# Cross attention, a state-space scan and experts on one core: first layers of three pairs ahead of the norm, and a first turn with its own order

## What is computed

```
x = x + xattn(hidden = ctx, z = layernorm(x))
x = x + ffn(layernorm(x))

xattn: xc = causal conv of 4 taps over (in_proj_w @ ctx);  u = silu(xc + conv_b)
       dt_lo, B, C = x_proj_w @ u
       delta = softplus(dt_proj_w @ dt_lo + dt_proj_b);  A = -exp(A_log)      # 16 states
       state = state * exp(delta * A) + (delta * u) * B;  y = sum_n state * C  # scan over 256 steps
       y = (y + D * u) * silu(z)
ffn:   shared = (sum over 2 experts of relu(x @ w1 + b1) @ w2 + b2) / 2
       routed = sum over 32 experts of gate * (relu(x @ w1 + b1) @ w2 + b2)    # width 176, top 6 of softmax
```

## Time and profile before

| | |
|---|---|
| median of 3 runs | 382.17 us |
| the profiled execution | 382.66 us, of which the span from first to last instruction is 380.8 |
| PE matmul busy | 354.3 us, 93% |
| DVE busy | 268.0 us, 70% |
| ACT busy | 218.9 us, 57% |
| POOL busy | 201.8 us, 53% |
| mean granted clock of PE | 0.978 of full speed |
| last product of batch 0's scan | starts at 54.61 us |
| first layer of pair 0, batch 0 | starts at 68.73 us |

### The profile page before, as it was taken

The page is one execution under the profiler, slowest core; times in us unless marked ns, Lnnn a source line. Parts: engine busy times, 40 slices in busy tenths (PEclk is TensorE's granted clock), DMA queues, the critical chain, the costliest instruction groups (busy, mean ns, idle before and its releaser), DMA issues.

```text
span 380.8 us, 6888 instructions
## 1 busy us (share of the span) xinstructions
PE 354.3 (93%) x2293; PEld 319.9 (84%) x2293; DVE 268.0 (70%) x455; ACT 218.9 (57%) x545; POOL 201.8 (53%) x159
## 2 busy tenths in 40 slices
PE   7437689999999999999999999999999998999997
PEld 4224367899999989999999899999999898999996
DVE  2579888999999547699977566899763645454454
ACT  2578764777864436477644446496424346665662
POOL 0289997178996102389962002799830033445442
PEclk9958899999999999999999999999999999999999
DMA  7498761159623223898322144964222144333310
GB/s 223 141 308 251 248 213 59 56 188 309 209 79 84 83 59 103 231 323 224 102 83 83 55 118 160 328 217 140 83 84 83 43 146 117 100 86 91 104 57 28
DMA packets 30825, 54.26 MB, mean 142 GB/s; under 512 B 3306, under 2 KB 8654, under 8 KB 30798
## 3 DMA queue, kind: packets, MB, share of 16 engines
q1 hardware_dynamic: 30798, 53.93, 46.9%
HBM read 52.60 MB, written 1.31 MB: 142 GB/s over the span
## 4 chain that ended last, share of the span: by engine, by line
PE 81%; DVE 8%; POOL 5%; issue 2%; ACT 2%; DMA 1%; SPq 0%; DVEq 0%; POOLq 0%; ACTq 0%
PE acc L552 36%; PE z L574 12%; PE z L576 11%; PE z L575 11%; PE dA L552 4%; POOL bu L957 3%; POOL w1l L937 2%; DVE dA L792 2%; PE misc L472 1%; DVE cv L756 1%; PE acc L450 1%; PE dA L486 1%; DMA ctxT<-in_ctx 1%; PE misc L526 1%; DVE b2F L776 1%
## 5 line engine op out<-in xcount | busy, mean ns | idle before, releaser
L552 PE MATMUL acc<-hg,w 128*128 128x256 f32 x564 | 133.5, 379 | 0.0
L712 ACT ACTIVATE z<-z,par 128x256 f32<-128x256 f32 x188 | 75.8, 439 | 82.8 <-PE z L576 82.5
L574 PE MATMUL z<-xh,w1l 128*128 128x256 f32 (+1 forms) x376 | 118.1, 314 | 0.0
L552 PEld LDWEIGHTS acc<-hg,w 128*128 128x128 f32 x564 | 102.4, 190 | 11.2
L957 POOL TENSOR_TENSOR bu<-bt,du 128x512 f32<-128x512 f32 x64 | 81.0, 1278 | 54.7 <-DMA bt<-bc 37.0
L894 DVE TENSOR_TENSOR hg<-z,gt 128x512 f32<-128x512 f32 x88 | 60.5, 688 | 64.9 <-ACT z L712 63.7
L576 PE MATMUL z<-xh,w1h 128*128 128x256 f32 (+1 forms) x376 | 106.2, 282 | 0.0
L575 PE MATMUL z<-xl,w1h 128*128 128x256 f32 (+1 forms) x376 | 105.9, 282 | 0.0
L792 DVE TENSOR_TENSOR_SCAN dA<-dA,bu 128x512 f32<-128x512 f32 x64 | 78.2, 1222 | 6.6 <-POOL bu L957 6.0
L574 PEld LDWEIGHTS z<-xh,w1l 128*128 128x128 f32 x376 | 71.2, 189 | 3.8 <-issue 2.2
L575 PEld LDWEIGHTS z<-xl,w1h 128*128 128x128 f32 x376 | 70.8, 188 | 1.6
(11 more groups left out here) (135 smaller groups left out, 410.0 us busy)
## 6 DMA issues: line engine op xcount, KB each, us to landing
w<-in_w SPq DMA_DIRECT2D x92, 256.0 KB, 2.8
bt<-bc SPq DMA_DIRECT2D x32, 256.0 KB, 5.0
ct<-bc SPq DMA_DIRECT2D x32, 256.0 KB, 5.7
stage<-in_w SPq DMA_DIRECT2D x11, 512.0 KB, 6.1
gt<-gates SPq DMA_DIRECT2D x14, 128.0 KB
xr<-in_xr SPq DMA_DIRECT2D x4, 256.0 KB, 6.1
x<-in_xT SPq DMA_DIRECT2D x4, 256.0 KB, 4.9
out<-x SPq DMA_DIRECT2D x3, 256.0 KB, 6.9
```

What stands on the lines that cost most here:

```text
L552: mm = pe.matmul(total(b, k), weights, h, start=t + n == 0 and (k == 0 or final_batch(b)), stop=last, skip_group_check=True)
L574: pe.matmul(z[p % ZB][:, i, :], w1l[:, t, one], xh_, start=k == 0, stop=False)
L712: ins = act.activation(z[p % ZB][:, i, :], z[p % ZB][:, i, :], ACT.Relu, bias=b1[:, t:t + 1])
```

## The change

- **First layers early.** For pairs 0 to 2 of batch 0 the first layer is computed from the centred xc, before the root of the variance is known (steps "xch" and "xcl" split it, "l1" is the first layer). When the root n2 is there, DVE multiplies z by it ("zr"), and the ReLU follows. Pair 3 is the first with the normed x.
- **Shared pairs.** For pairs 0 and 1 of every batch ACT writes hg itself (scale 1/2 and a halved bias b1s); DVE's product falls away.
- **The loop is written out.** run() goes over all batches and pairs. Turn 0 has a table of its own, TURN0; the units stand beside pairs 3 to 15 (UNIT_AT), two of them beside pairs 6, 10 and 13. The copying part of "turn" is a step of its own, "gates_out": beside pair 6 in batch 0. b2 is added behind second layer 6 there instead of 4.
- **Head.** Four products of batch 0 (POOLED) go from DVE to POOL, with their states in hg. The lower parts of w1 chunks 2 to 5 (BY_PE) are made by PE, identity times stage minus identity times w1h, in z1 and z2, and copied to w1l by ACT ("w1p", "w1e"). The first row pair of B is broadcast by PE ("rows") and ACT ("bt0") instead of through DRAM. delta of batch 0 is made in two halves; nb1 goes to ACT; the sum over the states of half k = 1 goes to misc, so that x1 of half 0 waits only for its own half. 39 fewer warm matmuls (of 78) stand before the norm.
- econv of batch 1 goes to the PSUM tile acc (e_of).

The core of the diff:

```diff
+EARLY = 3
 B2_AT = 4
+B2_AT0 = 6
 GLOW_AT = 2
+GLOW_AT0 = 6
 SINGLE0 = NP - NPR
 
 
 BURING = 4
+POOLED = [3, 6, 8, 11]
+BY_PE = [2, 3, 4, 5]
...
 BACK = [("yfold", 16), ("x1", 17), ("x1s", 18), ("mean", 19), ("centre", 19), ("sq", 19), ("sqs", 19), ("var", 20), ("r2", 20), ("norm", 20), ("logits", 21),
-        ("xh", 21), ("xl", 21), ("top", 21), ("ex", 22), ("gates", 22), ("turn", 23)]
-THIS = UNITS + ZGATE + BACK
+        ("xh", 21), ("xl", 21), ("top", 21), ("ex", 22), ("gates", 22), ("turn", 23), ("gates_out", 23)]
 NEXT = [("xin", 14), ("cv0", 15), (("taps", 1, KC), 16), ("econv", 17), ("uclip", 17), ("usig", 18), ("u", 19), ("xall", 20),
         ("dtl", 21), ("dt", 21), ("sp", 22), ("over", 22), ("delta", 23)]
-BEHIND = ("var", "logits", "xall", "dt", "turn")
+TURN = [(n, at, 1) for n, at in UNITS + ZGATE + BACK] + [(n, at, 2) for n, at in NEXT]
+BEHIND = ("var", "logits", "xall", "dt", "turn", "spread")
+AHEAD = [("xall", 1), ("var", 1)]
+
+
+UNIT_AT = [3, 4, 5, 6, 6, 7, 8, 9, 10, 10, 11, 12, 13, 13, 14, 15]
+TURN0 = [(("bu", 0, 0), 2, 1), (("bu", 0, 1), 2, 1)]
+for _c in range(NC):
+    for _k in range(KD):
+        _u = 2 * _c + _k
+        TURN0 += [(("decay", _c, _k), max(UNIT_AT[_u] - 1, 3), 1), (("scan", _c, _k), UNIT_AT[_u], 1), (("prod", _c, _k), UNIT_AT[_u], 1)]
+        TURN0 += [(("bu", (_u + 2) // 2, _k), UNIT_AT[_u], 1)] if _c + 1 < NC else []
+        TURN0 += [(("fold", _c, _k), UNIT_AT[_u], 1)]
+TURN0 += [("stats", 4, 1), ("rs1", 5, 1), ("nb1", 6, 1), ("zz", 7, 1), ("ez1", 8, 1), ("ez2", 9, 1), ("ez3", 10, 1), ("zmul", 12, 1),
+          ("xin", 15, 2), ("cv0", 15, 2), ("yfold", 15, 1), (("taps", 1, 2), 16, 2), ("x1", 16, 1), ("x1s", 16, 1),
+          (("taps", 2, 3), 17, 2), (("taps", 3, KC), 17, 2), ("econv", 17, 2), ("uclip", 18, 2), ("usig", 18, 2), ("u", 19, 2),
+          ("mean", 20, 1), ("centre", 20, 1), ("sq", 20, 1), ("sqs", 20, 1), ("xall", 20, 2), ("var", 21, 1), ("dtl", 21, 2), ("dt", 21, 2),
+          ("r2", 21, 1), ("norm", 21, 1), ("xh", 22, 1), ("logits", 22, 1), ("xl", 22, 1), ("sp", 22, 2), ("over", 22, 2), ("top", 22, 1),
+          ("ex", 23, 1), ("gates", 23, 1), ("delta", 23, 2), ("turn", NP, 1), ("gates_out", NP, 1)]
...
 HEAD = [(("warm", None, 11), 0), ("xin", 0), (("warm", None, 16), 0), ("cv0", 0), (("taps", 1, KC), 0), (("warm", "conv_done", 6), 0), ("econv", 0), ("uclip", 0),
-        (("warm", "uclip_done", 8), 0), ("usig", 0), ("b2h", 0), ("w1h", 0), ("w1l", 0), (("warm", "usig_done", 4), 0), ("u", 0), ("stats", 0), ("b2l", 0), ("xall", 0),
-        ("dtl", 0), ("b2s", 0), ("w1h", 0), ("w1l", 0), ("dt", 0), ("sp", 0), ("over", 0), ("rs1", 0), ("w1h", 0), ("delta", 0), ("nb1", 0)]
+        (("warm", "uclip_done", 8), 0), ("usig", 0), ("b2h", 0), ("w1h", 0), ("w1l", 0), (("warm", "usig_done", 4), 0), ("minus", 0), ("u", 0), ("stats", 0), ("b2l", 0), ("xall", 0),
+        ("dtl", 0), ("b2s", 0), ("w1h", 0), ("w1l", 0), ("dt", 0), ("rows", 0), ("sp", 0), ("over", 0), ("bt0", 0), ("delta", 0)]
 HEAD += [(("bu", 0, _k), 0) for _k in range(KD)]
 for _c in range(NC):
     HEAD += [(("decay", _c, _k), 0) for _k in range(KD)]
     HEAD += [(("bu", _c + 1, _k), 0) for _k in range(KD)] if _c + 1 < NC else []
-    HEAD += [("w1l", 0)] if _c in (1, 3, 5, 6, 7) else []
-    HEAD += [(n, 0) for n in ((), (), ("zz",), ("ez1",), ("ez2",), ("ez3",), ("zmul",), ())[_c]]
-    HEAD += [("w1h", 0)] if _c in (1, 2, 4, 5) else []
+    HEAD += [("w1l", 0)] if _c == 7 else []
+    HEAD += [("w1p", 0)] if _c in (1, 2, 4, 5) else []
+    HEAD += [("w1e", 0)] if _c in (2, 3, 5, 6) else []
+    HEAD += [(n, 0) for n in (("rs1", "nb1"), (), ("zz",), ("ez1",), ("ez2",), ("ez3",), ("zmul",), ())[_c]]
+    HEAD += [("w1h", 0)] if _c in (0, 1, 2, 4, 5) else []
     HEAD += [("xin", 1), ("cv0", 1)] if _c == NC - 1 else []
     for _k in range(KD):
         HEAD += [(("scan", _c, _k), 0), (("prod", _c, _k), 0)]
     HEAD += [(("sum", _c - 1), 0)] if _c else []
-HEAD += [("w1h", 0), ("w1l", 0), (("warm", None, 12), 0), (("sum", NC - 1), 0), ("w1h", 0), ("w1l", 0), ("w1h", 0), ("w1l", 0),
+HEAD += [("w1h", 0), ("w1l", 0), (("sum", NC - 1), 0), ("w1h", 0), ("w1l", 0), ("w1h", 0), ("w1l", 0),
          (("taps", 1, 2), 1), (("warm", None, 22), 0), ("w1h", 0), ("x1", 0), ("mean", 0), (("warm", None, 13), 0), (("taps", 2, 3), 1),
-         ("centre", 0), ("sq", 0), ("w1l", 0), (("taps", 3, KC), 1), ("var", 0), ("econv", 1), ("uclip", 1), ("r2", 0),
-         (("warm", None, 31), 0), ("norm", 0), ("usig", 1), ("xh", 0), ("logits", 0), ("w1h", 0), ("w1l", 0), ("u", 1), ("xl", 0),
-         ("top", 0), ("ex", 0), ("xall", 1), ("gates", 0), ("dtl", 1)]
-OPEN = [[("dt", 1), ("sp", 1), ("over", 1), ("delta", 1)],
-        [("spread", 0), ("turn", 0)],
-        [("acc_free", 0)] +
-        [(n, 1) for n in (("bu", 0, 0), ("decay", 0, 0), ("bu", 0, 1), ("decay", 0, 1), ("bu", 1, 0), ("scan", 0, 0), ("prod", 0, 0),
-                          ("decay", 1, 0), ("bu", 1, 1), ("scan", 0, 1), ("prod", 0, 1), ("decay", 1, 1), ("scan", 1, 0),
-                          ("prod", 1, 0), ("fold", 1, 0), "stats")]]
+         ("centre", 0), ("sq", 0), ("xch", 0), ("w1l", 0), (("taps", 3, KC), 1), ("xcl", 0), ("var", 0), (("warm", None, 4), 0),
+         (("l1", 0), 0), (("l1", 1), 0), (("l1", 2), 0), ("econv", 1), ("w1h", 0), ("w1l", 0),
+         ("uclip", 1), ("r2", 0), ("norm", 0), (("zr", 0), 0), ("usig", 1), ("xh", 0), ("logits", 0), ("xl", 0), ("u", 1),
+         ("top", 0), (("zr", 1), 0)]
+OPEN = [[("ex", 0), ("gates", 0), (("zr", 2), 0)],
+        [("dtl", 1)],
+        [("gt0", 0), ("sp", 1), ("over", 1), ("delta", 1)],
+        [("xall", 1), ("dt", 1), ("spread", 0)],
+        [],
+        [("turn", 0)],
+        [("gates_out", 0)]]
...
+            def beside(b, p):
+                due = list(OPEN[p]) if first(b) and p < len(OPEN) else []
+                for i in range(B - 1):
+                    due += [(n, i + d) for n, at, d in (TURN if i else TURN0) if i * NP + at == b * NP + p and i + d < B]
+                return due
 
             for name, b in HEAD:
                 step(name, b)
-            for p in range(SKEW):
-                pair(0, p, OPEN[p])
-            with eng.Fori(0, B - 2) as i:
-                for p in range(SKEW, NP):
-                    pair(i, p, beside(i, p))
-                for p in range(SKEW):
-                    pair(i + 1, p, beside(i + 1, p))
-            for p in range(SKEW, NP):
-                pair(B - 2, p, beside(B - 2, p, later=False))
-            for p in range(SKEW):
-                pair(B - 1, p, [])
-            for p in range(SKEW, NP):
-                pair(B - 1, p, [])
+            for b in range(B):
+                for p in range(NP):
+                    pair(b, p, beside(b, p))
...
-            load_bc(1, 0)
-            load_bc(1, 1)
+            for c in range(BRING):
+                load_bc(1, c)
             for b in range(B):
                 eng.wait_ge(S["gates_done"], b + 1)
                 eng.dma_start(gates_d[b % 2], gT[0:NR, :]).then_inc(S["spilled"], 16)
                 eng.wait_ge(S["spilled"], 16 * b + 16)
                 if b:
-                    eng.wait_ge(S["hg_done"], (b - 1) * NP + SINGLE0 + NPART)
+                    wait_hg(eng, b - 1, SINGLE0 + NPART - 1)
                     load_gates(b, 0)
-                    eng.wait_ge(S["hg_done"], b * NP)
+                    wait_hg(eng, b - 1, NP - 1)
                 load_gates(b, 1)
                 for p in range(NP):
-                    if b == 0 and p < 2:
-                        load_bc(1, 2 + p)
                     if 0 < b < B - 1 and p < BRING - 1:
...
+            lower = list(BY_PE)
+
+            def lower_w1(i):
+                pe.wait_ge(S["minus_done"], 1)
+                pe.wait_ge(w1h_done, i + 1)
+                if BY_PE.index(i):
+                    pe.wait_ge(w1e_done, BY_PE.index(i))
+                high = w1h[:, i * WCH:(i + 1) * WCH, :].rearrange("p t m -> p (t m)")
+                for h in range(2):
+                    for j in range(2):
+                        part = slice((2 * h + j) * L, (2 * h + j + 1) * L)
+                        pe.matmul(z[1 + h][:, j, :], ident, stage[:, i % WRING, part], start=j == 0, stop=False, skip_group_check=True)
+                    for j in range(2):
+                        part = slice((2 * h + j) * L, (2 * h + j + 1) * L)
+                        mm = pe.matmul(z[1 + h][:, j, :], minus[:], high[:, part], start=False, stop=True, skip_group_check=True)
+                mm.then_inc(S["w1p_done"], 1)
+
             def step(name, b):
-                if name[0] == "sum":
+                if name == "w1p":
+                    lower_w1(lower.pop(0))
+                elif name[0] == "l1":
+                    if name[1] == 0:
+                        pe.wait_ge(S["xcl_done"], 1)
+                    first_layer(name[1], xh[:, 1], xl[:, 1])
...
+                elif name == "rows":
```

(69 more changed lines are left out.)

165 lines of the change are left out of this document (104 added, 61 removed).

## The result

The changed kernel takes 388.52 us (median of 4 runs, 388.24 to 389.55) where the kernel before takes 382.17 (381.36 to 382.26, 4 runs): a ratio of 1.0175, 95% interval 1.0163 to 1.0187. The forecast was 385.9 with a range of 380.5 to 389.0, and "slower" with a chance of 0.75. The profiled execution took 388.61 us with a span of 386.8, so 6.0 more than the span of before.

The account below looks back on a forecast made before the run. TensorE's stream, busy 93% of the span, was taken as the bound. -0.65 (head) - 4.16 (to second layer 6) + 6.6 (w2 wait) + 0.24 (b2) + 1.7 (clock) = +3.7 on 382.17 gives 385.9 us, range 380.5 to 389.

Parts of the forecast that it names:

- C: Mark from which times are counted: the end of "centre" of batch 0, at 60.85 us in the kernel before.
- head, up to C: Start of batch 0 up to the end of "centre": 0.65 us earlier, with ACT's sum of work carrying it.
- C to second layer 6, unhindered: Batch 0 from C to the second layer of pair 6, without the weight wait: 4.16 us earlier than now.
- wait for w2 of pair 6: TensorE waits ahead of second layer 6 of batch 0 for its late weight load: 6.6 us, bounds 5.0 to 7.8.
- b2 and clock: b2 moved behind second layer 6 adds 0.24 us; half clock after the weight wait adds 1.7, bounds 0 and 2.8.
- the order on ACT: gates_out stands behind ReLU 6, decay 4 and product 2, so gates_done comes at C + 30.1 and delays the load.
- the bound of 2.0: Quickest landing time in us taken for the pair 6 w2 load, giving the low wait of 5.0; 2.8 was assumed.
- the walk: Unit-by-unit pricing of the batch 0 head: last decay ready at 51.8, last product at 54.7, C earlier by 0.65.
- The price of 1.0 for a half clock that lasts one stretch longer: Upper bound for the head: C comes 1.0 us later if the half clock lasts one stretch more.
- it costs nothing more: Coupling recurs at units 9 and 13, costing DVE some 2 us each, but hg of pair 14 comes when PE asks.
- rival one: The w2 load for pair 6 comes in time, so no wait: -4.6 us, 377.6 us; chance 0.13.
- Small moves and the loop: hg of pairs 0 and 1 on ACT, the bt(0,0) row by PE and ACT, and the written-out loop: nothing gained.

Follow-up runs that it names:

- experiment 1: Changed kernel with the w2 loads of pairs 6 to 8 of batch 0 issued by SP before the gates transfer; 389.86 us, ratio 1.0221.
- experiment 2: Changed kernel with decays 4, 9 and 13 of batch 1 listed on ACT under their own pair; 382.88 us, ratio 1.0033.
- experiment 7: Kernel of experiment 2 without the early first layers of pairs 0 to 2, warm matmuls in their place; 387.57 us, ratio 1.0117.
- experiment 8: Kernel of experiment 2 with all 16 products of the head on DVE, none on POOL; 388.48 us, ratio 1.0181.
- experiment 5: Kernel of experiment 2 with DVE's chain to u of batch 2 taken forward, u in pair 18 instead of 19; 383.52 us, ratio 1.0028.
- experiment 4: Kernel before the change with only its loop over two batches written out; 382.02 us, ratio 0.9999.
- experiment 10: Kernel of experiment 9 with 50 more warm matmuls ahead of the first lower part of w1; 381.01 us, ratio 0.9976.
- experiment 9: Kernel of experiment 6 with 12 warm matmuls behind sum(3) in the head; 381.35 us, ratio 0.9981.
- experiment 11: Kernel of experiment 9 without the early first layers of pairs 0 to 2; 385.89 us, ratio 1.0074.
- experiment 3: Changed kernel with both the w2 loads ahead of the gates and the three decays under their own pair; 384.23 us, ratio 1.0080.
- experiment 6: Kernel of experiment 5 with the w2 loads of pairs 6 to 8 issued ahead of the gates; 381.61 us, ratio 0.9991.
- experiment 12: Kernel of experiment 9 with all 16 products of the head on DVE; 383.02 us, ratio 1.0025.

## Why the prediction was right, and where it was not

The time is 2.6 us above the forecast of 385.9. The terms of the sum, in the profiled executions (C as in the prediction; after, C is 58.46 + 0.70 = 59.16):

| term | forecast | measured | from |
|---|---|---|---|
| head, up to C | -0.65 | -1.69 | 60.85 to 59.16 |
| C to second layer 6, unhindered | -4.16 | -3.82 | 95.33 to 89.82, less the head |
| wait for w2 of pair 6 | +6.6 | +8.17 | idle ahead of 97.99 |
| b2 and clock | +0.24 + 1.7 | +1.68 | 4.84 instead of 3.16 to second layer 7 |
| up to here | +3.7 | +4.34 | 102.83 against 98.49 |
| wait for u of batch 2 | 0 | +2.2 | second layer 18, 142.74 against 136.19 |
| wait behind the gates of batch 1 | 0 | +0.9 | 164.37 against 156.95 |
| batches 1 to 3 | 0 | -1.4 | 219.14 against 220.57 |

**What held.** The forecast hinged on the order on ACT: gates_out behind a ReLU, behind a decay, behind product 2. Product 2 was due at C + 27.35 and ended at C + 27.6; gates_done was due at C + 30.1 and came at C + 30.3; second layer 3 was due at C + 20.8 and came at C + 21.1. The shape too: a hole ahead of second layer 6, the gates sent 12.2 us behind du of batch 1, half clock behind it. Only the releaser was named otherwise, hg instead of the DMA, and experiment 1 shows that it was the DMA.

**The size of the wait.** SP was quicker than taken (load issued at C + 33.2, not 34.2), the load slower. It was given 2.8 us by the median in the earlier trace rows; it took 5.5. The five w2 loads issued from 92.3 to 98.4 take 5.5, 6.7 and 7.0 us (min, median, max). This could have been read before: in the trace of the kernel before, the load of pair 6 itself, issued at 81.99 among the broadcasts of B and C, took 6.6 us, and all seven of 80 to 100 a median of 5.8. The median over 96 loads was the wrong row, and the bound of 2.0 too. But the broadcasts behind the load don't set its time alone: with the same transfers issued behind it, the first five at the same distances, it took 3.0 us in experiments 2 and 7, 4.5 in 8 and 5.1 in 5. Why is open.

**The head.** Forecast -0.65, measured -1.69, of which 0.70 lies ahead of the first delta (20.61 to 19.91; it starts between 19.3 and 20.1 in the changed kernels and at 20.06 in the kernel of experiment 4, so this part is mostly no effect of the change) and 0.99 in the scan. So the walk was near, and its reason stood the test of experiment 10 (ACT, not the half clock in the first lower part). The price of 1.0 for a half clock that lasts one stretch longer holds: 0.55 in experiment 9, 0.95 in 5. What the bound left out is a second stretch in the queue ahead of a sum, 1.6 more in experiments 5 and 7.

**The step that failed** is "it costs nothing more". The prediction saw that decays 9 and 13 repeat the coupling and cost DVE some 2 us each (measured: idle 2.28 and 1.17, beside 2.19 for pair 6). It then asked only whether hg of pair 14 comes late, and didn't follow DVE's chain to its end, u of batch 2, on which xall hangs. Before, u is done at 130.75 and TensorE asks for it at 133.67: 2.9 us to spare, less than the change takes out of TensorE's stream (5.5 at second layer 6), while du is no earlier than before (77.29 against 75.67). Hence rival one (377.6 if the load comes in time) could not have come true with this order: experiment 1 removes the load's wait, and the time stays. The prediction's number was near because two limits of nearly the same length lay one under the other and it had found one of them. That much of it is luck: the +6.6 stands for a wait that is really there but doesn't set the end of the turn, in the place of a limit that the prediction didn't see.

**Small moves and the loop.** Nothing, as forecast: experiment 4, 0.9999.

**What stays open.** From batch 1 on, all changed kernels take 219.1 us between the marks and both forms of the kernel before 220.6 to 220.9. Of the 1.4 us 1.0 lies in batch 3, where the second layer is split: most of its second layers lie 2.86 apart before, and 2.78 and 2.84 in turn after. In batches 1 and 2 they lie 3.15 apart instead of 3.16. It is not the loop and not the chip (experiments 1, 2 and 4 ran on the same one). What makes the matmuls quicker I haven't found. The wait for x of batch 0 at batch 1 (0.7 to 1.3 in every changed kernel) was not tried: gates_out of batch 1 stands under pair 0 of the next batch there.

**A version that beats both.** Decays beside their own pair, u early, w2 first, warm matmuls in the head (experiment 10): 381.01, 0.24% below the kernel before (interval 0.13% to 0.35%) and 2.0% below the changed kernel by the ratios (0.9976 against 1.0175). It keeps every part of the change. How much of the profit is the early layers' isn't shown (experiment 11).

## What to carry to other kernels

When a change pulls the bounding engine's stream forward, write down for each other engine's chain how much it had to spare before; the gain at that point is capped by the smallest of these (here 2.9 us at u), and a hole that you find may hide a second limit as long as itself. Take one hole away at a time and look where the end of the chain behind it lies, not only whether the hole is gone. In an in-order queue, an entry that waits for the same step's work of another engine passes its wait to everything behind it: three entries moved by one place were worth 5.4 us, more than the early layers or POOL's share of the products brought here. And take the price of a transfer from the row of that very transfer, not from the median of its kind: 6.6 us against 2.8.

## What the runs showed of the hardware

- The same head runs with a first stretch at half clock of 10.2 us (18.9 to 29.1, changed kernel) or 13.7 us (17.7 to 31.3, experiment 5), and with or without a second one. A wait of TensorE of 1.95 us (experiments 5 and 7) was followed by a second stretch of 3.4 us, one of 1.50 in the same place (changed kernel, experiments 1, 2, 3 and 6) was not, and, behind 12 warm matmuls, neither was one of 1.86 (experiment 12). The longer first stretch moves the end of the head by 0.55 to 0.95 us, the second one by 1.6. In other places too equal waits differ: one of 3.38 us was followed by half clock in experiment 3 and not in experiment 1 (1.00 from 139.5 to 144), one of 1.8 in experiment 6 and not in experiment 9 (1.00 from 94 to 120).
- The load of w2 of pair 6 (256 KB) took 5.5 us in the changed kernel and 6.6 in the kernel before, against a median of 2.8 over the run. With the changed kernel's order of transfers around it, it took 3.0 us in experiments 2 and 7, 4.5 in 8 and 5.1 in 5.
- Filling a hole with warm matmuls cost nothing that shows: 12 of them (1.47 us) stand in the hole of experiment 10, whose centre is at delta + 38.56, and there are none in the changed kernel, where it is at delta + 38.55.
